# Routing and scattering for three tree networks moved into the attention stage of a fused Trainium2 kernel, row maxima handled two heads at a time

## The reference

```
# layer 1: attention in a window of 64, 16 heads of 16
scores = exp(scores - max(scores, axis=-1, keepdims=True))   # max over all 1024 keys
scores = where(mask, scores, 0.0)                            # -32 <= j - i <= 31
weights = softmax(scores, axis=-1)                           # again, over all keys
x = layernorm(x + (weights @ v) @ Wo)

# layer 2: q, k and v come from three tree networks (fff) with their own weights
def fff(x, node_w, node_b, w1, b1, w2, b2):      # depth 4, 15 nodes, 16 leaves, 64 hidden
    cur = 0
    for _ in range(4):
        cur = 2 * cur + 1 + (x @ node_w[cur] + node_b[cur] >= 0)
    leaf = cur - 15
    return relu(x @ w1[leaf] + b1[leaf]) @ w2[leaf] + b2[leaf]
x = layernorm(x + softmax(q @ k.T / 16) @ v)     # one head of 256, within a batch
```

## Time and profile before

| | us |
|---|---|
| median of three runs | 2375.14 |
| profiled execution, device time | 2370.24 |
| its span in the trace | 2368.4 |
| first part, up to the second part's first instruction | 1287.6 |
| from there to the first leaf tile's transposes | 180.9 |
| leaf tiles | 404 |
| gathers and attention of the second layer | 496 |

### The profile page before, as it was taken

One profiled execution on the slowest core, in us unless ns is written; L12 is line 12 of the kernel. 1 busy time (PEld: TensorE's weight loads), 2 busy tenths in 40 slices (PEclk: granted clock), 3 DMA queues, 4 the chain that ended last, 5 costly groups with the idle time before them and its releaser, 6 DMA issues. The chain is left out here.

```text
span 2368.4 us, 43674 instructions
## 1 busy us (share of the span) xinstructions
PE 2010.5 (85%) x14301; PEld 1580.6 (67%) x14301; DVE 1608.7 (68%) x4115; ACT 1364.3 (58%) x2463; POOL 775.2 (33%) x1133
## 2 busy tenths in 40 slices
PE   3679999999999999999994883474688669999998
PEld 1346667666666666666663883464688659999997
DVE  2667787787877878788752455376597647777775
ACT  2568788877787878888861221253476434444442
POOL 4112122212222222223011355546502175555511
PEclk9889999999999999999997555788799979999999
DMA  2566654567545575454712716999987533333311
GB/s 55 78 94 86 87 86 85 96 104 107 76 82 94 98 123 70 83 99 65 124 38 68 233 69 215 383 380 286 338 259 260 192 96 98 95 99 98 90 41 39
DMA packets 227755, 306.04 MB, mean 129 GB/s; under 512 B 41373, under 2 KB 143562, under 8 KB 227146
## 3 DMA queue, kind: packets, MB, share of 16 engines
q1 hardware_dynamic: 182906, 198.35, 40.5%
q0 software_dynamic: 24320, 67.92, 9.0%
q10 hardware_dynamic: 20304, 36.97, 4.1%
HBM read 129.33 MB, written 92.27 MB: 94 GB/s over the span
## 5 line engine op out<-in xcount | busy, mean ns | idle before, releaser
L774 DVE CUSTOM_DVE_ANT_0 above<-p_half,above 128x512 f32<-128x512 f32 x1024 | 681.3, 684 | 208.7 <-ACT above L669 168.5
L669 ACT ACTIVATE above<-p_diff 128x512 f32<-128x512 f32 x1024 | 585.0, 602 | 160.3 <-PE p_diff L565 137.9
L565 PE MATMUL p_diff<-d_stack,q_stack 96*128 96x512 bf16 x1024 | 394.1, 387 | 69.5 <-ACT above L669 50.9
L569 PE MATMUL p_half<-k_stack,q_stack 96*128 96x512 bf16 x1024 | 389.1, 383 | 5.2 <-DVE row_max L774 3.2
L611 PEld LDWEIGHTS p_pv<-v_win,w_win 128*128 128x128 f32 x2048 | 283.1, 192 | 25.4 <-issue 0.4
L611 PE MATMUL p_pv<-v_win,w_win 128*128 128x34 f32 x2048 | 291.1, 268 | 0.0
L565 PEld LDWEIGHTS p_diff<-d_stack,q_stack 96*128 96x128 bf16 x1024 | 137.8, 136 | 193.3 <-ACT above L669 143.0
L1209 POOL DMA_INDIRECT raw<-sorted_y,place x192 | 202.2, 1053 | 193.9 <-DMA sorted_y<-y_tile 138.1
L1531 ACT ACTIVATE pt_hi<-p_one 128x512 fp32r<-128x512 f32 x128 | 69.5, 595 | 253.2 <-PE p_one L1391 253.2
L450 POOL TENSOR_TENSOR att<-total,inv 128x128 f32<-128x128 f32 x128 | 48.7, 400 | 445.9 <-DVE inv L800 445.9
L684 ACT ACTIVATE w_win<-p_win 128x512 f32<-128x512 f32 x256 | 153.0, 598 | 54.2 <-PE p_win L587 41.6
(11 more groups left out here) (228 smaller groups left out, 5012.0 us busy)
## 6 DMA issues: line engine op xcount, KB each, us to landing
x_tile<-sorted_x SPq DMA_DIRECT2D x141, 256.0 KB, 4.8
sorted_y<-y_tile ACTq DMA_DIRECT2D x141, 256.0 KB, 4.2
q_stack<-q_parts SPq DMA_DIRECT2D x256, 96.0 KB, 3.1
k_stack<-k_parts SPq DMA_DIRECT2D x256, 96.0 KB, 3.7
x_in<-in_L_attn_x SPq DMA_DIRECT2D x16, 1024.0 KB, 6.6
x_rows<-x POOLq DMA_DIRECT2D x16, 1024.0 KB, 9.9
sorted_x<-zeros SPq DMA_DIRECT2D x51, 256.0 KB, 9.2
d_stack<-d_parts SPq DMA_DIRECT2D x256, 48.0 KB, 3.6
```

Of the source, the lines that this page charges most:

```text
L565: nc.tensor.matmul(p_diff[s % 2][:], qs, d_stack[0:SPLIT_ROWS, h, :], start=True, stop=True).then_inc(s_diff, 1)
L569: nc.tensor.matmul(p_half[s % 3][:], qs, k_stack[g][0:SPLIT_ROWS, h, HALO + S // 2:HALO + S], start=True, stop=True).then_inc(s_half, 1)
L669: nc.scalar.activation(above[:, s % 4], p_diff[s % 2][:], ACT.Relu).then_inc(s_above, 1)
L774: nc.vector.tensor_tensor_reduce(out=above[:, s % 4], in0=p_half[s % 3][:], in1=above[:, s % 4], scale=1.0, scalar=-3.0e38, op0=ALU.add, o ...
```

## The change

- Tensors that both parts use live in a new class `Shared`. Its `y`, two batches of rows, holds the output product, residual and normalised rows of a batch, and its `scatter` sends 128 rows of `y` for one net.
- All routing moves into the first part: new jobs R0 to R3 transpose the normalised rows of a batch and split them (`rt_hi`, `rt_lo`); `node_scores` multiplies them with the nodes at steps 42, 58, 74 and 90; `decide` and `tree` follow on VectorE, one operation of the tree per step; job K0 counts ranks in `p_job`; `slots` follow three to five steps later. From step 60 of unit (b + 2, 0) on GpSimd issues one scatter of batch b every fourth step, 24 for the three nets. The last batch's 24 scatters are issued at the start of the second part.
- The second part has no routing, no x1 loads for it, and no scatters other than these 24.
- The maxima of two heads at a time are transposed (`MAX_AT`), split and stored: four times a unit, not once. The window work starts at step 29 after the scores of its head and not at step 76.
- `q_stack` and `k_stack` have one copy each. The load of a head for the next unit waits for its window scores in the current one.
- Jobs start at the steps of a table `START`. The projections of the next unit begin at step 28 (before: step 13). Normalising is at steps 20 to 27 of the second unit of a batch. GpSimd, not SyncE, issues `v_win`.
- Net 0's weights are split after the tables and no longer between the batches of the routing.

```diff
+JOBS = {
+    0: ["V0", "V1", "V2", "R3", "V3", "V4", "S0", "q0", "q1", "k0", "k1", "d0", "T0", "T1", "K0", "X0", "X1"],
+    1: ["O0", "O1", "O2", "O3", "X2", "X3", "R0", "q0", "q1", "k0", "k1", "d0", "T0", "T1", "R1", "R2"],
+}
...
+START = {
+    0: [0, 4, 8, 12, 16, 20, 24, 28, 32, 36, 40, 44, 45, 49, 53, 57, 61],
+    1: [0, 4, 8, 12, 16, 20, 24, 28, 32, 36, 40, 44, 45, 49, 53, 61],
+}
+MAX_AT = (18, 34, 50, 66)
...
-WIN_LAGS = (12, 14)
+WIN_LAGS = (29, 31)
...
-SPREAD_AT, NORM_FIRST = 4, 7
+SPREAD_AT, NORM_FIRST = 18, 20
+NODES_AT = (42, 58, 74, 90)
+TREE_AT, SCATTER_AT, SCATTER_EVERY = 27, 60, 4
...
-                wait_alone(sp, s_win, GH * (u - 1) + h + 1)
+                wait_alone(sp, s_win, GH * u + h + 1)
...
+                    for r, n, t in scatters(b, g, s):
+                        pool.wait_ge(s_slot, r + 1)
+                        keep.scatter(pool, r, n, t, s_scat[r % 2])
...
+            def max_rows(w, i, k):
+
+                pool.wait_ge(s_mrest, k + 1)
...
+                wait(pool, s_win, GH * (w - 1) + 2 * i + 2)
+                alone(pool)
+                for part in range(3):
+                    row = SPLIT_ROWS + part
+                    pool.dma_start(q_stack[row:row + 1, 2 * i:2 * i + 2, :],
+                                   m_parts[:, part, :]).then_inc(s_mrow, 16)
...
+            def node_scores(r, i, k):
+
+                pe.wait_ge(s_jdone, before(ALL_JOBS, *route_job(r, i)) + 1)
+                wait(pe, s_e1, 2 * heads_before(nodes_start(r, i)))
+                wait(pe, s_go, k)
+                for t in (0, 1):
+                    cols = slice(P * t, P * t + P)
+                    for c in (0, 1):
+                        ins = three(p_node[:, 48 * t:48 * t + 48], rt_hi[:, c, cols], rt_lo[:, c, cols],
+                                    node_hi[:, c, :], node_lo[:, c, :], c == 0, c == 1)
+                ins.then_inc(s_rn, 1)
...
-                if half == 0 and h == 0:
-                    pe.wait_ge(s_mrow, 48 * (w + 1))
+                if half == 0 and h % 2 == 0:
+                    pe.wait_ge(s_mrow, 48 * (4 * w + h // 2 + 1))
...
-                        if n == 0:
-                            sp.wait_ge(s_first, 16 * QT * B)
-                        else:
-                            for half in (0, 1):
-                                sp.wait_ge(s_scat[half], 16 * QT * (B // 2) * n)
+                        sp.wait_ge(s_scat[n], 16 * QT)
...
-            for k in range(2 * B):
-                if 1 < k + 1 < 2 * B:
-                    again(k + 1)
-                pool.wait_ge(s_xagain[k % 2], 16 * (k // 2 + 1))
-                scatter(1 + k // B, k % B, x_in[k % 2], s_scat[k % 2])
+                    keep.scatter(pool, B - 1, n, t, s_scat[n])
```

More of the change, by code:

```diff
@@ L60, in present, with before @@
         "O": 1 <= b <= B,
-    }[kind]
-def counted(kinds, b, g, j):
+        "R": 1 <= b <= B if g == 1 else 2 <= b <= B + 1,
+        "K": 2 <= b <= B + 1,
+    }[name[0]]
+def before(kinds, b, g, j):
     n = 0
-    for bb in range(-1, B + 1):
+    for bb in range(-1, B + 2):
         for gg in (0, 1):
@@ L240, in has_scores, with batches @@
-        def has_scores(b):
-            return not isinstance(b, int) or 0 <= b < B
-        def job_at(step, lag):
-            s = step - 1 - lag
-            return s // 4 if s >= 0 and s % 4 == 0 else None
+        def batches(unit):
+            for b in range(-1, B + 1):
+                for g in (0, 1):
+                    unit(b, g)
+            unit(B + 1, 0)
         def jobs(b, g, step, lag):
-            j = job_at(step, lag)
-            if j is not None and j < len(JOBS[g]):
+            if step - lag in START[g]:
+                j = START[g].index(step - lag)
@@ L616, in weighted_values @@
                     ins.then_inc(s_pv, 1)
-            batches(pe, unit)
+            batches(unit)
         @block.scalar
@@ L854, with leaf_attention @@
 GROUP = 16
-def leaf_attention(nc, x1, nets, out):
+def leaf_attention(nc, x1, nets, out, keep):
     with ExitStack() as ctx:
@@ L1673, in _ @@
                 assert done == TAB_NET[n]
+            for k in range(PIECES):
+                piece(0, k)
             placed = 0
@@ L1814 @@
     out = nc.dram_tensor("out_0", (B, S, C), F32, kind="ExternalOutput").ap()
-    window_attention(nc, *(aps[n] for n in _IN1), x1)
-    leaf_attention(nc, x1, [[aps[n] for n in _IN2[6 * i:6 * i + 6]] for i in range(NETS)], out)
+    nets = [[aps[n] for n in _IN2[6 * i:6 * i + 6]] for i in range(NETS)]
+    with ExitStack() as ctx:
+        keep = Shared(nc, ctx)
+        window_attention(nc, *(aps[n] for n in _IN1), nets, x1, keep)
+        leaf_attention(nc, x1, nets, out, keep)
     return run_bass_kernel_spmd(nc, [arrays], core_ids=[0]).results[0]["out_0"]
```

756 lines of the change are left out of this document (360 added, 396 removed).

## The result

The changed kernel takes 2213.27 us (median of four runs, 2212.3 to 2214.36) against 2373.47 us before; the ratio is 0.9312, 95% interval 0.925 to 0.9375. The forecast was 2215 us. That the two agree to 2 us is luck: the total hides larger misses in its terms, which cancel. The profiled execution has a span of 2210.5 us, 157.9 less than before.

A forecast was written before the change was run, and what follows sets the result against it. The prediction took TensorE to bound the first part and a chain of small dependent steps the second part's start; 2368.4 + 49.5 - 3 - 137 - 67 = 2211, 2213 with 1.8 around it, forecast 2215 us, range 2150 to 2290.

The forecast's parts named there:

- Added TensorE work in the first part, +10 a batch: First part: added products and transposes 8.6 us plus VectorE 1.4 us a batch, unhidden; +65 us in all.
- 1.4 us for VectorE's crowded steps: First part, steps 16 to 31 of a batch's second unit: VectorE becomes longest of three engines by about 1.4 us.
- Rival 1: First part: TensorE's 97% is no bound, additions vanish and cost nothing; 2165 us, chance 0.13.
- Give-back, -16: First units: later q0 removes 16 of 27 us of ScalarE's waits to write q_parts.
- Drain, -3: Between last scores and second part: earlier window work saves 17 us, last batch's routing costs about 14.
- Start, -137: Second part up to the first tile transpose: 180.9 us shrinks to 44.1 with routing gone.
- Tiles, -67: Leaf tiles: 404 us becomes 337 without scatters of nets 1 and 2 and reloads beside them.
- Net 1 starts without a gap: Leaf tiles: expected sign that net 1 no longer waits for its scatters; tiles at 2.2 to 2.4 us.
- bound of -93: Leaf tiles: largest saving, with 2.17 us a tile throughout and net 0's wait for weights gone.
- 2: First part: single stacks make a new ring, ScalarE's q0 copy waits every unit; +52 us, 2265, chance 0.15.
- 3: Leaf tiles: limited by their own transfers, scatters a bystander; saving only 25 us, 2255, chance 0.08.
- 4: First part: TensorE waits for maxima chains four times a unit; 155 us, all the rest saves, chance 0.03.

The follow-up runs named there:

- node_third: Changed kernel with routing's node products cut to one of three, 16 instead of 48 per batch; 2186.65 us, ratio 0.9209 to the kernel before.
- before_more_products: Kernel before with each transpose of jobs T and X made three times, 64 more per batch; 2398.84 us, ratio 1.0122.
- tiles_loaded: Changed kernel plus sixteen x1 reloads and 128 scatters into unread tensors beside the leaf tiles; 2331.4 us, ratio 0.9679 to the kernel before.
- weights_on_pool: Changed kernel with weights of nets 1 and 2 issued by GpSimd, not SyncE; 2238.76 us, ratio 0.928 to the kernel before.
- best: Changed kernel with shorter drain and GpSimd issuing weights of nets 1 and 2, net 1's after the first tile transpose; 2198.35 us, ratio 0.9275.
- after: Profile of the changed kernel itself; 2213.27 us, ratio 0.9312 to the kernel before.
- after_again: Changed kernel unaltered, run again as yardstick on the third chip; 2213.46 us, ratio 0.9331 to the kernel before.
- maxima_two_later: Changed kernel with transposes of the maxima two steps later (20, 36, 52, 68); 2231.47 us.
- maxima_six_later: Changed kernel with transposes of the maxima six steps later (24, 40, 56, 72); 2369.03 us, ratio 0.9971 to the kernel before.

## Why the prediction was right, and where its steps were not

The direction and the large terms hold, with the causes of the largest, the start of the second part. That the time agreed to 2 us is luck: the first part was put 33 us too high, and drain, start and tiles together 34 us too low.

- **Added TensorE work in the first part, +10 a batch:** mis-sized, 6.0. The products cost their start distance, as said and as node_third shows, but "none of it is hidden while TensorE is 97% busy" was wrong: before_more_products finds 2.7 to 3.9 us a batch of cover in the kernel before. The 1.4 us for VectorE's crowded steps did not show: at full clock the second unit of a batch, which has these steps, grew from 70.7 to 73.8 us, and the first from 73.3 to 76.7. Rival 1 was thus true to about a third.
- **Give-back, -16:** the first four units became 16.8 us shorter net of their additions, with 26.8 us of waits gone, so somewhat too cautious.
- **Drain, -3:** +13.7, the step that failed worst. Up to the end of the statistics the drain was 10 us shorter by the earlier window work, where I had 17. Behind them it is 23.6 us longer (31.1 and not 7.5), where I took 14 for the last batch's routing, from tree steps and hand-overs. The four pieces with single buffers take 5.1 us each at a granted clock of 0.55, so the routing ends 28.1 us after the statistics. GpSimd's 18 scatters of the seventh batch and the 7.9 us behind them, which the prediction had not put there at all, end 3.0 us later still.
- **Start, -137:** -132.9. The first 16 zeroing transfers were issued over 23.3 us, and over 14.9 before; the last batch's scatters run beside them, but that these are the cause was not tested.
- **Tiles, -67:** -53.7. Net 0 without its stall, 110.4 us for 47 tiles, is 2.35 us a tile, where 2.4 was taken. "Net 1 starts without a gap" failed, and by a wrong reading of the trace before: the wait in net 1 was for SyncE's queue with the weights of net 2 in it, not for the scatters, so it stayed, at 20.7 us. The stated bound of -93 was also a slip: 404 - 141 x 2.17 is 98.
- **Rivals:** 2 did not occur, 3 is excluded by tiles_loaded, 4 did not occur, but a transpose six steps later would have cost the whole gain, by the chain, the shared bank and a lower clock together. Two edits priced at nothing matter if done otherwise: v_win's queue is worth 43 us, and the place of the transposes 18 us (two steps) to 156 us (six).

## What to carry to other kernels

A serial stage can be hidden in an earlier one even if that one's bound engine is 97% busy: here 181 us became 48 for 30 us more in and behind the busy part, and it pays to measure an engine's real cover by repeating cheap instructions, as its busy share does not give it. A wait for a loaded tile does not say why the load was late: look at what stands ahead of it in its queue. In this case the scatters that were blamed had landed before 1598.33 us, and the wait ended at 1666.23, behind a burst of weights. Where two chains run side by side, as routing and scatters do in the drain, shortening one gives only the distance to the other. A place in an order table is a price: count for each shared bank who must have read it, and for each queue which late step its last entry waits for. When a variant is slower by more than its waits, compare busy time and granted clock before the waits are blamed for all of it.

## What the runs showed of the hardware

- TensorE, 97% busy by the trace with 490 of 726 us of weight loading, took in 7.1 us more per batch for 3.2 us (4.4 between stretches at full clock); once this was used, each product of 48 columns cost 0.104 to 0.111 us. The Trainium skill, "Perfetto Trace Analysis", section on identifying the most-contended engine, calls matmul busy time a poor measure and asks for the share of weight loading (and for the share of peak work). The runs agree that 97% busy does not give the headroom, but the third of free time, which the share of weight loading suggests, was not there either.
- Weights of a net, issued by SyncE over 9.7 to 12.3 us between tile loads, held the tiles for 13.9 and 20.7 us, and for 21.8 and 27.6 us in the kernel before, with scatters beside them. From GpSimd's queue these two stalls are gone, but some 45 to 60% of their time did not come back (weights_on_pool: 34.7 us of stalls, 18.9 gained; best: 35.4 and 13.6).
- The second part started 7.9 us after GpSimd's last scatter in each of the four profiles in which that scatter ended last (after, after_again, node_third, maxima_two_later), in node_third although VectorE's slots had been ready for 9.5 us.
- With the same TensorE instructions, ten units of maxima_six_later kept TensorE busy for 796 us at a mean granted clock of 0.92, and 739 us at 1.00 in the changed kernel.
